# Perceiver block on one core: when a batch's keys, values and queries are prepared

## The reference

```python
x = x + xattn(layernorm(x), ctx, ctx)   # 16 query heads of 32, ONE key/value head of 32 for all
x = x + attn(layernorm(x), Ww, Wr, ..)  # gated linear recurrence in chunks of 64, 4 heads of 128
x = x + ffn(layernorm(x), Wg, w1, w2)   # 16 experts, one per row, capacity 128; 512 -> 2048 -> 512

# xattn
Q = (q @ Wq + bq);  K = k @ Wk + bk;  V = v @ Wv + bv
attn = softmax(Q K^T * 32**-0.5);  out = (attn @ V) @ Wo + bo
# attn, per chunk: A = inv(eye - A0), A0 from products of normalized rows with a decay
# ffn: softmax gate, argmax expert, rows past an expert's capacity give zero
```

## Time and profile before

| | us |
|---|---|
| median of 3 runs | 2423.58 (2422.32 to 2427.81) |
| profiled execution, its own time | 2427.98 |
| its span, first to last instruction | 2426.1 |
| PE busy | 2189.4 (90%) |
| DVE, ACT, POOL busy | 1371.0, 1193.3, 1638.2 |
| attention iterations 2 to 14, each | 117.2 to 118.1 |
| experts, from about 2007 on | about 419 |

### The profile page before, as it was taken

How to read it: one execution, slowest core, us unless ns; L and a number is a source line. 1 busy time by engine, 2 the same in 40 slices (tenths; PEclk the granted TensorE clock), 3 DMA queues, 4 the chain that set the end, 5 groups by cost and what they waited for, 6 DMA issues and landing times. The chain is left out here.

```text
span 2426.1 us, 35019 instructions
## 1 busy us (share of the span) xinstructions
PE 2189.4 (90%) x12608; PEld 1429.9 (59%) x12608; DVE 1371.0 (57%) x2311; ACT 1193.3 (49%) x2237; POOL 1638.2 (68%) x1323
## 2 busy tenths in 40 slices
PE   5889898989998989898989898989898769999999
PEld 3435555546464646464646464645554448999998
DVE  2665757566667566666666666666665433333333
ACT  3555554646464646464645455555554313333333
POOL 0676878677777777777777777777777714655655
PEclk9889998999899989998999899989998889999999
DMA  4532120202020202121211111121120009999995
GB/s 160 188 113 66 40 82 24 83 23 83 23 83 23 83 26 80 40 66 40 66 47 58 51 59 63 43 66 42 59 79 9 18 14 375 350 363 346 362 363 189
DMA packets 108157, 263.75 MB, mean 109 GB/s; under 512 B 9849, under 2 KB 35065, under 8 KB 99792
## 3 DMA queue, kind: packets, MB, share of 16 engines
q1 hardware_dynamic: 98448, 235.32, 27.7%
q10 hardware_dynamic: 5952, 14.29, 1.6%
q0 software_dynamic: 3584, 11.90, 1.2%
HBM read 223.74 MB, written 25.72 MB: 103 GB/s over the span
## 5 line engine op out<-in xcount | busy, mean ns | idle before, releaser
L917 POOL TENSOR_TENSOR psum<-psum,p 128x512 f32<-128x512 f32 x896 | 1162.9, 1298 | 291.7 <-ACT p L553 197.7
L708 DVE TENSOR_REDUCE mpart<-bank 128x1 f32<-128x512 f32 x1024 | 675.0, 682 | 403.5 <-PE bank L357 396.1
L553 ACT ACTIVATE p<-bank 128x512 f32<-128x512 f32 x1024 | 596.8, 600 | 553.5 <-PE bank L370 543.6
L357 PE MATMUL bank<-kT,qT 96*128 96x512 f32 x1024 | 484.1, 480 | 62.6 <-DVE mpart L708 32.5
L370 PE MATMUL bank<-qT,kT 97*128 97x512 f32 x1024 | 502.4, 492 | 4.7 <-ACT p L553 4.0
L357 PEld LDWEIGHTS bank<-kT,qT 96*128 96x128 f32 x1024 | 199.6, 196 | 211.5 <-DVE mpart L708 104.6
L370 PEld LDWEIGHTS bank<-qT,kT 97*128 97x128 f32 x1024 | 201.7, 197 | 142.6 <-issue 113.6
L382 PE MATMUL bank<-p,v 128*32 128x512 f32 x2048 | 271.4, 651 | 0.0
L1159 POOL TENSOR_TENSOR w2l<-w,w2h 128x1024 fp32r<-128x1024 f32 x64 | 203.2, 3177 | 75.1 <-PE ebank L1074 54.4
L332 PE MATMUL bank<-cst,w_first 128*128 128x128 f32 x1024 | 164.1, 287 | 21.7 <-DMA w_first<-in_ctx 18.0
L332 PEld LDWEIGHTS bank<-cst,w_first 128*128 128x128 f32 x1024 | 134.3, 149 | 64.9 <-issue 29.4
(11 more groups left out here) (159 smaller groups left out, 3137.8 us busy)
## 6 DMA issues: line engine op xcount, KB each, us to landing
w<-in_w SPq DMA_DIRECT2D x48, 2048.0 KB, 20.1
w_first<-in_ctx SPq DMA_DIRECT2D x64, 1024.0 KB, 4.9
w_first<-in_w SPq DMA_DIRECT2D x16, 2048.0 KB, 11.6
dispatched<-route ACTq DMA_DIRECT2D x17, 513.0 KB, 4.4
dis<-dispatched SPq DMA_DIRECT2D x16, 513.0 KB, 3.5
qT<-qh SPq DMA_DIRECT2D x128, 64.0 KB, 2.0
xin<-in_x SPq DMA_DIRECT2D x16, 256.0 KB, 2.6
qT<-qs SPq DMA_DIRECT2D x64, 64.0 KB, 2.0
```

Of the source, the lines that this page charges most:

```text
L357: e.matmul(a[:], qT[b % 2][0:3 * HD, (4 * g + h) * P:(4 * g + h + 1) * P], kT[b % 2][0:3 * HD, c * 512:(c + 1) * 512], start=True, stop=Tr ...
L553: e.activation(p[n % NP][:], B_BANK[u % 2][:], ACT.Exp).then_inc(p_act.sem, 1)
L708: e.tensor_reduce(mpart[g % 2][:, n:n + 1], A_BANK[(17 * g + n) % 2][:], AX.X, ALU.max).then_inc(max_dve.sem, 1)
L917: e.tensor_tensor(acc[:], first[:], p[(UNITS * b + u) % NP][:], ALU.add).then_inc(psum_pool.sem, 1)
```

## The change

Numbers and order change; no computation does. Every instruction of the kernel before stands in the changed one, with the same operands.

- The context tiles come every 6 ticks, from tick -19 to tick 71, where they came every 4, from 8 to 68. A negative tick lies in the iteration before: -19 is tick 109. Key/value chunks move from 23, 39, 55, 71 to 4, 28, 52, 76.
- x is normalized, transposed and projected at ticks -62 to -34, that is 66 to 94 of the iteration before (was 1 to 30 of its own). The query quarters stand four ticks apart. The queries are sent at tick 2, once the scores of two batches earlier have been read from that tile.
- All loops start at i = -2, and each iteration also calls `prepare(i + 2, t - TICKS)`.
- Two waits on KV_BANK follow the new order. `sums` waits for the first chunk of batch b + 2 (was: the last of b + 1), and the second chunk, not the first, waits for the reciprocals. The first chunk waits for the queries (`q_dve`), and the queries for the last chunk of the batch before.
- The counters of `finish` are split in `post_*` and `late_*`, so that its late steps could run in a further iteration; with TAIL = 0 they stand where they stood, and the ticks of POST, now written out as lists, are the same.

```diff
-NORM, XN, XNT, QPROJ, QSEND = 1, 5, 10, 27, 38
-TILE_AT = [8 + 4 * k for k in range(KB)]
-KV_AT = [TILE_AT[4 * c + 3] + 3 for c in range(4)]
-VT_AT = [KV_AT[2 * m + 1] + 7 for m in range(2)]
-LOAD_AT = [t + 6 for t in TILE_AT[3::4]]
+NORM, XN, XNT, QPROJ, QSEND = -62, -58, -51, [-46, -42, -38, -34], 2
+TILE_AT = [6 * k - 19 for k in range(KB)]
+KV_AT = [TILE_AT[4 * c + 3] + 5 for c in range(4)]
+VT_AT = [38, 82]
+LOAD_AT = [t + 4 for t in TILE_AT[3::4]]
...
             def send_queries(b):
+                if b >= 2:
+                    e.wait_ge(*b_pe.at(b - 2, UNITS - 1))
...
             def sums(b):
...
-                if b + 1 < B:
-                    e.wait_ge(*kvs_dve.at(b + 1, 3))
+                if b + 2 < B:
+                    e.wait_ge(*kvs_dve.at(b + 2, 0))
...
-                if t == QPROJ:
-                    if b == 0:
-                        e.wait_ge(*wq_in.at(0))
-                    e.wait_ge(*kvs_dve.at(b, 0))
-                    e.wait_ge(*xnT_act.at(b))
+                if t in QPROJ:
+                    m = QPROJ.index(t)
+                    if m == 0:
+                        if b == 0:
+                            e.wait_ge(*wq_in.at(0))
+                        else:
+                            e.wait_ge(*kvs_dve.at(b - 1, 3))
+                        e.wait_ge(*xnT_act.at(b))
...
-                    if c:
-                        e.wait_ge(*kvs_dve.at(b, c - 1))
-                    elif b:
-                        e.wait_ge(*(o_dve.at(b - 2, "recip3") if b > 1 else kvs_dve.at(0, 3)))
-                    if c == 1:
-                        e.wait_ge(*q_dve.at(b))
+                    e.wait_ge(*(kvs_dve.at(b, c - 1) if c else q_dve.at(b)))
+                    if c == 1 and b >= 2:
+                        e.wait_ge(*o_dve.at(b - 2, "recip3"))
...
-            for i in range(-1, B + 1):
+            for i in range(-2, B + 2):
...
-                for t in range(TICKS):
+                for t in range(TICKS if i <= B else TAIL):
...
-                    if i + 1 < B:
+                    if 0 <= i + 1 < B:
                         prepare(i + 1, t)
+                    if i + 2 < B:
+                        prepare(i + 2, t - TICKS)
```

More of the change, by code:

```diff
@@ L190, in attention @@
         o_dve = named("o_dve", "recip0 recip1 recip2 recip3 att")
[L193 to L197, removed]
+        post_pe = named("post_pe", "x1 xn2T V rkT I X1")
+        post_act = named("post_act", "ss0 ss1 ss2 ss3 xn2T rk0 rk1 rk2 rk3 V rkT X1")
+        post_dve = named("post_dve", "x1 st2 mv2 xn2 XT1a MT IT")
+        post_pool = named("post_pool", "xb ve2 rs2 x12 rm rn MT0 XT0 XT1")
+        late_pe = named("late_pe", "Vn oT2 x2 xn3T lg loc")
+        late_act = named("late_act", "Vn oT2 xn3T eg")
+        late_dve = named("late_dve", "x2 st3 mv3 xn3 lg0 lmax emax cand best oh ohloc before loc valid locc row0 row "
+                         "d0 d1 sidx gate token token1")
+        late_pool = named("late_pool", "ve3 rs3")
         y_pe, z_pe, xt_pe = count("y_pe", LEVELS), count("z_pe", LEVELS), count("xt_pe", LEVELS - 1)
@@ L301, in _ @@
                         send_max(b, g)
-                    if t in LOAD_AT:
+                    if t in LOAD_AT and i >= -1:
                         c = LOAD_AT.index(t) + 2
@@ L305, in _ @@
                             load_ctx(i + 1 + c // 4, c % 4)
-                    if t == 0 and i >= 1:
+                    if t == 0 and 1 <= i <= B:
                         if i > 1:
-                            e.wait_ge(*post_pe.at(i - 2, "Vn"))
+                            e.wait_ge(*late_pe.at(i - 2, "Vn"))
                         else:
@@ L311, in _ @@
                         e.dma_start(xr[:], T["x"][i - 1]).then_inc(xr_in.sem, 16)
-                    if t == POST["store"] and i >= 1:
-                        e.wait_ge(*post_dve.at(i - 1, "x2"))
-                        e.dma_start(T["out"][i - 1], x2).then_inc(x2_out.sem, 16)
+                    for b, at in ((i - 2, t + TICKS), (i - 1, t)):
+                        if at == POST["store"] and 0 <= b < B:
+                            e.wait_ge(*late_dve.at(b, "x2"))
+                            e.dma_start(T["out"][b], x2).then_inc(x2_out.sem, 16)
                     if t == LOAD_AT[3] and i == LAST - 1:
@@ L830, in finish @@
[L830 to L840 removed]
+                        late_dve.sem, 1)
@@ L970, in _ @@
                     e.wait_ge(*zeroed.at(ZEROES - 1))
-                for t in range(TICKS):
+                for t in range(TICKS if i <= B else TAIL):
                     if 0 <= i < B and t % 2:
                         add_weights(i, t // 2)
-                    if i + 1 < B:
+                    if 0 <= i + 1 < B:
                         prepare(i + 1, t)
-                    if i >= 1:
+                    if i + 2 < B:
+                        prepare(i + 2, t - TICKS)
+                    if i >= 2:
+                        finish(i - 2, t + TICKS)
+                    if 1 <= i <= B:
                         finish(i - 1, t)
```

242 lines of the change are left out of this document (128 added, 114 removed).

## The result

The changed kernel takes 2477.1 us, median of 4 runs (2472.06 to 2479.22), against 2425.69 for the kernel before on the same chip (4 runs, 2422.32 to 2428.54). The ratio is 1.0209, 95% interval [1.0186, 1.0232]: slower by 2.1%, where 2364 us was forecast. The closest case was rival 1 (2474), and only a part of what it named is what happened.

What follows compares the result with a forecast made beforehand. PE was taken to bound most of each iteration, DVE part of A. Steady iterations (-45.5), iteration 14 (-9.2) and the first iterations (-5) gave -60 us, 2368; 4.4 less for the median gave 2364, range 2325 to 2404.

Steps and rivals of the forecast that it cites:

- rival 1: Moved work brings a new wait, chunk at tick 4 ahead of the reciprocals: +3.9 us per iteration, about 2474; chance 0.08.
- 3.8 us of PE work goes from B: Per steady iteration, PE gives -3.8 us in B and +0.9 in A, -2.9 us together.
- B: Rest of the iteration, from the first x1 matmul: 88.3 us, where PE was said to set the pace.
- A: Stretch from the x2 addition near tick 107 to x1's first matmul at next tick 15: 29.5 us, PE busy 23.6.
- rival 2: Latency, not PE's work, sets B; only half the steps at iterations 0 and 14 remain: about 2417; chance 0.10.
- Idle time in B, -0.6: Queries at ticks 82 to 94 cover short gaps of the level chain: -0.6 us per iteration, bounds +1.5 and -4.2.
- Clock, 0: The slow spell behind the stall for `turned` stays: 0 us per iteration, bounds -1.5 and +1.5.
- a rival on the fast side alone: PE stays at 2.4 GHz, most idle time filled: -7.5 us per iteration, 2309; chance 0.07 beyond the forecast.
- DVE in A, 0: Work leaving and arriving ahead of the reciprocals cancels, so they stay as late: 0 us, bounds -1.0 and +0.8.
- Iteration 14, -9.2: No next x, queries or first four tiles to prepare, 5.7 us, with the steady 3.5: -9.2 us.
- Iterations 0 and 1, -5: POOL is fed about 7 us sooner, shortening PE's 6.5 us wait at the sums: -5 us, bounds 0 and -6.5.
- Prologue, 0: Earlier query sends and fourth tile group stand against the next batch's work: 0 us, bounds -4 and +4.

Runs made afterwards that it cites:

- E10: The changed kernel with its first key/value chunk at tick 14 instead of 4: 2452.55 us.
- E1: The changed kernel with its first key/value chunk back at tick 23 instead of 4: 2408.91 us.
- E2: The kernel before with only x and the queries moved into the iteration ahead, tiles and chunks as before: 2423.76 us.
- E3: The changed kernel with x and queries back in their own iteration (quarters at ticks 20 to 24), tiles spread, first chunk at 4: 2398.61 us.
- E4: The changed kernel with 12 more identity transposes per iteration, at ticks 22 and 26, whose result nobody reads: 2441.87 us.
- E9: E3 with the first key/value chunk at tick 14 instead of 4: 2372.2 us.
- E5: E1 with the weights of later stages loaded at tick 63 of iteration 0 instead of tick 2: 2404.58 us.
- E7: E1 with the context tiles of ticks 17 and 23 moved ahead of x1, to 13 and 15: 2421.04 us.
- E6: The changed kernel with the chunk at tick 4 split into four steps at ticks 4 to 7: 2519.14 us.

## Why the prediction was wrong, by its steps

- **"3.8 us of PE work goes from B, where PE sets the time, into A, where it has 5.9 us to spare": this step failed.** The first part of A did take its four tiles, better than the +0.9 forecast: 12.2 us before and after, PE's idle time there from 1.6 to 0.8. The second part, of which I said "it fits", got 2.2 us longer and PE's idle time rose from 3.7 to 4.8. What is idle there is a wait with DVE's row behind it, and the chunk stands behind that wait in PE's list, ahead of the scores that DVE needs next. Idle time summed over a stretch is not room for work at a given tick. E10, with the chunk still in A but at tick 14, is 25 us faster.
- **"PE sets the pace" of B, so that work taken out is time won: failed as well, and cost most.** B has its own latency hole in ticks 19 to 27. The change took the chunk, a tile and the first query quarter out of it: B went from 89.4 to 90.6 us, not down by 4.4, which is 5.6 of the 6.9 us between forecast and result of a steady iteration. PE's busy time in B fell by 0.6 us only, not 3.8: the low level there rose from 4.8 to 9.8 us, worth 2.5. Rival 2 had this mechanism, but let it only cancel the gain. E1 and E2 (chunk at 23) and E3 (queries at 20 to 24) show that either filler suffices; E4 shows the clock's part of the price, and E1 is 44 us faster than E10, which has the chunk at 14 and the hole open.
- **Idle time in B, -0.6:** +1.8, past the bound of +1.5.
- **Clock, 0:** 3.6 us more per iteration at the low level (B +5.0, A less), worth 1.8, just past the bound of +1.5. Before, the clock record has two low stretches per iteration, one around its start and one some 15 us in; now there is a third, some 33 us in, behind the hole. I had counted the one behind `turned` alone. The Trainium skill (TensorE: Matmul & The Clock Gate, "What's actually happening") has sustained activity as the condition of the fast state; E4, faster with more work, agrees. I used it for a rival on the fast side alone, when it speaks as much against thinning out a stretch.
- **DVE in A, 0:** its busy time up to x1 fell by 0.6 us, near the 0.75 of the working, but its idle time there rose from 0.7 to 3.5 on average, and x1 comes 2.2 us later; this is what rival 1 said of the freed 2.4 us. The bound of +0.8 was also added up wrongly: with the long form and nothing hidden its own rows give 0.75 + 1.24 + 1.63 - 2.4 = +1.2. The long form of `kT`, rival 1's other price, went the other way: one of 64 is above 1.0 us after the change, 14 of 64 were before. What sets it, which the prediction left open, the records show (last section).
- **Right:** ticks 80 to 96 are 3.1 longer (forecast 4); the wait for `turned` stays at 2.3; the sums' wait for `kvs` at tick 9 costs nothing in the steady iterations; iteration 15 is no slower (101.9 us against 105.3). Ticks 16 to 80 are 1.9 us shorter, not 9: the 2.6 us won in ticks 32 to 64 are all that B gave.
- **Iteration 14, -9.2:** +1.1. The absent queries and x save 3.7 in ticks 64 to 96, the absent tiles 0, the hole is still there, and no steady gain comes on top.
- **Iterations 0 and 1, -5:** the wait for `psum` fell from 6.5 to 1.9, and iteration 1 is 3.2 us shorter, but iteration 0 is 7.8 longer; it has waits of 8.4 us for the maxima's transfer, which it did not have before.
- **Prologue, 0:** +5.8, past the bound of +4. I reckoned SP's issues and some 3 us of the next batch's work; the projection ahead of the first tile, 6.49 us, wasn't costed.

E9 takes 3.3 us off an iteration, nearly the -3.5 forecast, but not as forecast: PE's idle time stays (9.4 to 9.1), and 3.0 us are busy time, most of it the clock's (low level 10.3 to 5.3 us). In none of the kernels in the table did PE's idle time fall by more than 0.4.

Open: how the slow spells are released. E9's one run at 2398 wasn't traced, but its mean granted clock was 0.945 against 0.958 to 0.960 in the others; some 65 us more at half the pace, an estimate from these figures, cost about 32 us and would account for the 26. The start of the changed kernel (13.6 us) goes with the early queries (E2 +16.5, E3 +0.5) and is only partly taken apart beyond that: E5 recovers 4.6.

## What to carry to other kernels

Before moving work out of a stretch where the bounding engine is "busy 95%", remove it on paper and walk the dependent chain through it: work that covers a latency is paid back twice when it leaves, as idle time and as a slower clock behind. Idle time on an engine can be used only by work that stands in its list ahead of the instruction that waits; work behind it holds up what the other engine needs next. And when two edits are combined, ask whether each alone relied on the other's instructions as filler: here 0 and -26 us made +51.

## What the runs showed of the hardware

- One list of instructions takes 114.3 or 120.7 us an iteration, by where the low clock level falls (E5). Within that run three kinds of iteration recur in a fixed order. The fastest and slowest runs of E7 lie 32 us apart, at mean granted clocks of 0.952 and 0.939, which by the estimate at E5 is the whole of it; for E5 the clock accounts for some 12 of its 32.
- 1.6 us of matmuls whose result nobody reads make each iteration 2.3 us shorter (E4).
- Two matmuls of 512 columns by themselves hold PE for 1.0 us, eight in a row for 1.94 (E6): parting the steps of this chunk doubled its price.
- DVE's low part of `kT` takes 1.5 to 1.6 us in 13 of 64 cases before, and 0.68 to 0.74 in 63 of 64 after (1.09 in one), with the same operands at other ticks. It depends on what POOL does when it starts. Before, the 14 cases above 1.0 us are those that began while an addition (`psum<-psum,p`) was running, and each ended 0.54 us after that addition did: with 0.49 us of it left the instruction took 1.03, with 1.07 left 1.62. In the 43 cases in which DVE began up to 0.4 us ahead of POOL, DVE took 0.68 and it was the addition that took 1.59 to 1.82 us instead of 1.27. After the change, 42 of 64 began within the last 0.05 us of an addition, so they lost next to nothing. In these traces the two exclude each other, and whoever starts first finishes first.
